# One of eight broadcast adds per pair of sequences on POOL instead of VectorE, with a copy of the keys in SBUF

## The reference, cut to what matters

```python
q = x @ Wq + bq
k = x @ Wk + bk
v = x @ Wv + bv
scores = einsum('d,bijd->bij', attn_scale, tanh(q[:, :, None, :] + k[:, None, :, :]))
weights = softmax(scores, axis=-1)
attn = einsum('bij,bjd->bid', weights, v)
attn = attn @ Wo + bo
x = layer_norm(x + attn, g1, beta1)
h = relu(x @ W1 + bf1)
x = layer_norm(x + h @ W2 + bf2, g2, beta2)
```

## Time and profile before

| | |
|---|---|
| median of three timed runs | 1179.35 us (1177.79 to 1180.16) |
| the profiled execution | 1169.94 us, its span 1168.1 us |
| pair stages (additive attention to routing) | from 0 to about 740 us |
| experts | about 760 to 1064 us |
| last stage | about 1064 to 1168 us |
| one turn in the loop, from one qT (406.54) to the next (447.44) | 40.90 us: DVE busy 35.59, PE 34.23, ACT 31.63, POOL 10.76 us |
| TensorE clock granted in that turn | 0.96 of full speed, mean of the span 0.909 |

### The profile page before, as it was taken

The page is one execution under the profiler, slowest core; times in us unless marked ns, Lnnn a source line. Parts: engine busy times, 40 slices in busy tenths (PEclk is TensorE's granted clock), DMA queues, the critical chain, the costliest instruction groups (busy, mean ns, idle before and its releaser), DMA issues.

```text
span 1168.1 us, 24664 instructions
## 1 busy us (share of the span) xinstructions
PE 872.7 (75%) x7427; PEld 665.8 (57%) x7427; DVE 708.7 (61%) x2209; ACT 667.8 (57%) x1643; POOL 392.2 (34%) x458
## 2 busy tenths in 40 slices
PE   3457889789778978987898887167766666665887
PEld 1235566556555655655665565166656656665787
DVE  4398878988898898889889643311211112123776
ACT  3266878777777877777787554033433434342343
POOL 7500111322331232233123333365655555551111
PEclk9978899999999999999998888578998998897999
DMA  8200000000000000000000000447766675665000
GB/s 196 29 1 1 1 8 2 8 8 0 7 7 7 0 7 7 0 7 7 7 0 8 8 8 8 90 131 212 210 183 193 182 196 169 179 185 112 14 17 21
DMA packets 53976, 71.08 MB, mean 61 GB/s; under 512 B 10818, under 2 KB 40624, under 8 KB 53936
## 3 DMA queue, kind: packets, MB, share of 16 engines
q1 hardware_dynamic: 45456, 62.56, 19.7%
q0 software_dynamic: 8480, 8.01, 3.0%
HBM read 64.17 MB, written 11.03 MB: 64 GB/s over the span
## 4 chain that ended last, share of the span: by engine, by line
PE 36%; issue 25%; DVE 19%; DMA 8%; another core or an unknown queue 5%; POOL 3%; SPq 2%; ACT 1%; DVEq 0%; POOLq 0%
PE b_s L1207 6%; DMA b2buf<-in_L_ffn_b 5%; PE big L1334 5%; PE b_o L1374 5%; DVE tbuf L794 5%; PE big L1486 4%; PE big L1324 4%; DVE spread L794 4%; POOL pr L424 2%; DVE pr L921 2%; PE b_qk L1501 2%; PE b_s L1501 2%; PE big L1361 1%; SPq L343 1%
## 5 line engine op out<-in xcount | busy, mean ns | idle before, releaser
L1486 PE MATMUL big<-hbT,wbuf 128*128 128x128 f32 x672 | 108.5, 312 | 91.7 <-DMA b2buf<-in_L_ffn_b 47.4
L794 DVE TENSOR_TENSOR tbuf<-qT,b_qk 128x2304 f32<-128x2304 f32 x64 | 162.7, 2547 | 19.6 <-remote 10.7
L657 ACT ACTIVATE act_h<-big,wbuf 128x128 f32<-128x128 f32 x336 | 95.7, 368 | 122.5 <-PE big L1486 75.7
L541 ACT ACTIVATE tbuf<-tbuf 128x2304 f32<-128x2304 f32 x64 | 135.6, 2119 | 46.6 <-DVE tbuf L794 38.4
L1486 PEld LDWEIGHTS big<-hbT,wbuf 128*128 128x128 f32 x672 | 94.0, 216 | 103.8 <-issue 50.7
L1207 PE MATMUL b_s<-tbuf,apad 128*32 128x192 f32 x1536 | 97.5, 393 | 59.4 <-ACT p L550 51.8
L1092 DVE TENSOR_SCALAR hbT<-b_t,cols 128x128 f32<-128x128 f32 x84 | 34.3, 409 | 147.8 <-PE b_t L1479 85.1
L482 POOL DMA_INDIRECT hrow<-tok_dram,igather x84 | 85.5, 1018 | 80.9 <-PE b_t L1479 37.4
L491 POOL DMA_INDIRECT eo_dram<-eo,iscatter x84 | 85.9, 1023 | 56.7 <-issue 32.7
L424 POOL TENSOR_TENSOR pr<-pr,rs 96x384 f32<-96x384 f32 x64 | 52.7, 824 | 149.5 <-DVE rs L928 149.5
L1207 PEld LDWEIGHTS b_s<-tbuf,apad 128*32 128x32 f32 x1536 | 51.0, 126 | 90.4 <-issue 48.8
(11 more groups left out here) (209 smaller groups left out, 1916.0 us busy)
## 6 DMA issues: line engine op xcount, KB each, us to landing
wbuf<-in_wpack SPq DMA_DIRECT2D x84, 514.0 KB
b2buf<-in_L_ffn_b SPq DMA_DIRECT2D x84, 64.0 KB
tok_dram<-tn SPq DMA_DIRECT2D x32, 96.0 KB
spread<-eo_dram SPq DMA_DIRECT2D x1, 2688.0 KB, 16.0
out<-of SPq DMA_DIRECT2D x16, 96.0 KB, 1.7
hrow<-tok_dram,igather POOLq DMA_INDIRECT x84
eo_dram<-eo,iscatter POOLq DMA_INDIRECT x84
tab_dram<-tid_now,slot_now POOLq DMA_INDIRECT x64
```

What stands on the lines that cost most here:

```text
L541: act.activation(v, v, ACT.Tanh).then_inc(s["tanh"], 1)
L657: last = act.activation(act_h[:, r % 2, c * TILE:(c + 1) * TILE], big[r % 2][:, c * TILE:(c + 1) * TILE], ACT.Silu, bias=wbuf[:, r, 2 * DF ...
L794: dve.tensor_tensor(ring[c % TRING].rearrange("p (x m n) -> p x m n", m=CQ, n=N), qv.unsqueeze(3).to_broadcast([D, SPLIT * QG, CQ, N]), kv ...
L1486: last = pe.matmul(big[r % 2][:, c * TILE:(c + 1) * TILE], wbuf[:, r, c * D:(c + 1) * D], hbT[:, r % 2, :], start=True, stop=True)
```

## The change

A new helper `add_chunk` writes the add for any engine and any copy of the keys. The last chunk of a pair, number 7 (LENT), goes to POOL. POOL can't read PSUM, so `qk_evac` first copies the keys to SBUF (`kT`). POOL's add stands right after `keep_x` in its body; it waits for the queries of its pair and for score 3, which frees its buffer. It counts on a semaphore of its own, `add_p`. The tanh of chunk 7 waits for that one, the other tanh for the DVE's count of seven a pair, and PE's `qk` and DVE's `qk_evac` wait for both.

```diff
--- before.py
+++ after.py
@@ -33,6 +33,7 @@
 CH = G * CPB
 CW = SPLIT * QG * CQ * N
 TRING = 4
+LENT = CH - 1
 DEPTH = 5
 VC = D + 2
 EPS_TOK, EPS = 1e-6, 1e-5
@@ -155,6 +156,7 @@
         xs = sb("xs", [N, G, D])
         xT = sb("xT", [D, TN])
         qT = sb("qT", [D, TN])
+        kT = sb("kT", [D, TN])
         bqk = sb("bqk", [D, 1])
         vrow = sb("vrow", [N, G, VC])
         nmax = sb("nmax", [128, SPLIT])
@@ -251,7 +253,7 @@
 
         s = {n: ctx.enter_context(nc.semaphore("s_" + n)) for n in [
             "ids", "ld_a", "ld_b", "late", "consts", "gate", "pool_c", "tab_init", "setup_mm", "setup",
-            "raw_mm", "raw_ev", "emb0", "emb1", "emb2", "xs", "kept", "xs_t", "xT", "qk", "qk_ev", "add", "tanh", "score",
+            "raw_mm", "raw_ev", "emb0", "emb1", "emb2", "xs", "kept", "xs_t", "xT", "qk", "qk_ev", "add", "add_p", "tanh", "score",
             "nmax", "exp1", "p1t", "p1T", "vp", "vp_ev", "att", "x1", "x1h", "x1_t", "x1T", "x1bT", "f", "f_ev", "y2",
             "x2", "h0_rows", "xa", "xa_t", "xaT", "hg", "hg_ev", "hv", "hv_ev", "s2", "s2_ev", "exp2", "rs2", "pn",
             "t2", "t2_ev", "o_init", "o", "h1n", "res", "tn", "tn_t", "hT", "r", "rT", "lg", "routed", "gap",
@@ -285,6 +287,17 @@
             return t[:, bass.ds(p, 1), :, :].rearrange("p a g d -> p (a g) d")
 
 
+        def add_chunk(eng, c, keys):
+
+            g, cc = c // CPB, c % CPB
+            qv = qT[:, g * N:(g + 1) * N].rearrange("p (x m) -> p x m", m=QM)[:, :, CQ * cc:CQ * cc + CQ]
+            kv = keys[:, g * N:(g + 1) * N]
+            return eng.tensor_tensor(
+                ring[c % TRING].rearrange("p (x m n) -> p x m n", m=CQ, n=N),
+                qv.unsqueeze(3).to_broadcast([D, SPLIT * QG, CQ, N]),
+                kv.unsqueeze(1).unsqueeze(1).to_broadcast([D, SPLIT * QG, CQ, N]), ALU.add)
+
+
         @block.sync
         def _(sp):
             def load(dst, src, sem):
@@ -409,6 +422,11 @@
                 pool.wait_ge(s["xs"], p + 1)
                 pool.tensor_copy(pair_of(res, p), xs[:, :, :]).then_inc(s["kept"], 1)
 
+            def add(p):
+                pool.wait_ge(s["qk_ev"], p + 1)
+                pool.wait_ge(s["score"], p * CH + LENT - TRING + 1)
+                add_chunk(pool, LENT, kT).then_inc(s["add_p"], 1)
+
             def root(p, n):
                 pool.wait_ge(s["var_" + n], p + 1)
                 pool.tensor_tensor(rstd[n][:, :], ve[n][:, :], neghalf[:, 0:G], ALU.pow)\
@@ -453,6 +471,7 @@
 
                 at(n, 1, root, "x1")
                 at(n, -1, keep_x)
+                at(n, 0, add)
 
                 at(n, 3, roots_h1)
                 at(n, 2, normalise, 0)
@@ -536,7 +555,10 @@
             act.preload_act_table(ACT.Exp)
 
             def tanh(p, c):
-                act.wait_ge(s["add"], p * CH + c + 1)
+                if c == LENT:
+                    act.wait_ge(s["add_p"], p + 1)
+                else:
+                    act.wait_ge(s["add"], p * (CH - 1) + c + 1)
                 v = ring[c % TRING]
                 act.activation(v, v, ACT.Tanh).then_inc(s["tanh"], 1)
 
@@ -782,20 +804,15 @@
 
             def qk_evac(p):
                 dve.wait_ge(s["qk"], p + 1)
-                wait(dve, s["add"], p * CH)
+                wait(dve, s["add"], p * (CH - 1))
+                wait(dve, s["add_p"], p)
+                dve.tensor_copy(kT[:, :], p_k)
                 dve.tensor_scalar(qT[:, :], b_qk[:, 0:TN], bqk[:, :], None, ALU.add).then_inc(s["qk_ev"], 1)
                 dve.wait_ge(s["qk_ev"], p + 1)
 
             def add(p, c):
                 wait(dve, s["score"], p * CH + c - TRING + 1)
-                g, cc = c // CPB, c % CPB
-                qv = qT[:, g * N:(g + 1) * N].rearrange("p (x m) -> p x m", m=QM)[:, :, CQ * cc:CQ * cc + CQ]
-                kv = p_k[:, g * N:(g + 1) * N]
-                dve.tensor_tensor(
-                    ring[c % TRING].rearrange("p (x m n) -> p x m n", m=CQ, n=N),
-                    qv.unsqueeze(3).to_broadcast([D, SPLIT * QG, CQ, N]),
-                    kv.unsqueeze(1).unsqueeze(1).to_broadcast([D, SPLIT * QG, CQ, N]), ALU.add)\
-                    .then_inc(s["add"], 1)
+                add_chunk(dve, c, p_k).then_inc(s["add"], 1)
 
             def x_rows(p):
                 if known(p) and p == 0:
@@ -1012,7 +1029,6 @@
                 at(n, 1, x1_norm)
                 at(n, 0, v_rows)
 
-                at(n, 0, add, 7)
                 at(n, 2, mask_max, 0)
 
                 at(n, 0, products)
@@ -1216,7 +1232,8 @@
 
             def qk(p):
                 pe.wait_ge(s["xT"], p + 1)
-                wait(pe, s["add"], p * CH)
+                wait(pe, s["add"], p * (CH - 1))
+                wait(pe, s["add_p"], p)
                 for i in range(2):
                     last = pe.matmul(b_qk[:, i * TN:(i + 1) * TN], wqk[:, i, :], xT[:, :], start=True, stop=True)
                 last.then_inc(s["qk"], 1)
```

## The result

| | before | changed kernel |
|---|---|---|
| median of four timed runs | 1179.76 us (1177.79 to 1182.27) | 1199.8 us (1194.96 to 1204.2) |
| the profiled execution | 1169.94 us | 1194.96 us |
| its span | 1168.1 us | 1193.1 us |
| mean granted TensorE clock | 0.909 | 0.887 |
| one turn in the loop, qT to qT | 40.90 us | 42.19 us |

The ratio is 1.0175, with a 95% interval of 1.0141 to 1.021: the change makes the kernel slower by about 20 us. The forecast was 1213.8 us, with a range of 1192 to 1238. Profile against profile the difference is 25.0 us, where the prediction summed 34.4.

What follows compares the result with a forecast made beforehand. The turn's path was taken to lie on PE up to `qk`, then on DVE. Stalls of `x1_norm` and `cums` of 30.35 us plus copies made 34.4 us, added to the 1179.35 us median: 1213.8 us, range 1192 to 1238.

Steps and rivals of the forecast that it cites:

- Add 7 is worth nothing: On PE's half of the turn: removing DVE's 2.54 us add only lengthens its 1.95 us wait to about 4.5 us.
- the adds are the bound after all: Rival, chance 0.04: DVE's add of chunk 7 would be on the path, its removal saving 2.27 us a turn, total 1145.
- the reading of the two halves of the turn: The turn's path lies on PE from the transposes behind `xa` to `qk`, then on DVE from the queries through adds 0 to 2.
- The copy, 15 x 0.27 = 4.05 us: On DVE between `qk` and the queries: copying the keys is all on the path, 0.27 us for each of pairs 1 to 15.
- POOL's add, 4.94 us: On POOL behind `keep_x`: the chunk's add sized as six times a 0.823 us operation of 384 values, hidden as work.
- the two bounds of 3.5 and 4.94: Length of POOL's add: 3.5 us from nine one-input copies of 0.39 us, 4.94 from six two-input operations of 0.823 us.
- x1_norm stands still until POOL is through: On DVE beside POOL's add: `x1_norm` takes some 3 us instead of 0.59, ending 0.34 us after the add.
- The term of 1.8 us a turn: PE starts `x1_turn` at 400.28 instead of 398.51 because `x1_norm` waits; turns 4, 6 to 14 and 15 give 19.8 us.
- Turn 5: POOL's add should start before the late `cums`, so `cums`, add 6 and `x1_norm` stand behind it: 4.4 us.
- POOL before `cums` in every turn: Rival, chance 0.11: POOL's add goes ahead of `cums` in turns 6 to 14 too, 23 us more, 1237.
- No stall: Rival, chance 0.12: `x1_norm` isn't held by POOL's add, so only the copies count: 1183.4 us.
- The clock falls in the new gap: Rival, chance 0.10: PE's clock falls after standing still 1.8 us before `x1_turn`, 2 us a turn, 22 more, 1236.

Runs made afterwards that it cites:

- POOL's add behind `x1_norm`: The changed kernel, with POOL's add also waiting until `x1_norm` of the turn is done: 1117.11 us, ratio 1.0014 to the kernel before.
- the same with the copy late: The changed kernel, with POOL's add waiting for `x1_norm` and for the keys' copy, which moves to where add 7 stood: 1112.69 us, ratio 0.9968 to the kernel before.
- Chunk 2's place: Against the kernel before, POOL adds chunk 2 instead of chunk 7, behind `roots_h1` and `slot_now`; DVE keeps chunk 7 and pair 0's chunk 2: 1157.51 us, ratio 0.9821.
- copy-only kernel: The kernel before plus the copy of the keys ahead of the queries, read by nobody; all eight adds stay on DVE: 1118.27 us against 1115.53, ratio 1.0036.
- the kernel with one input in PSUM: The changed kernel, with the roots copied to PSUM and `x1_norm` reading them there in another operation: 1182.59 us, ratio 1.0052 to the kernel before.
- the kernel that adds twice: The changed kernel, with POOL doing its add twice over the same buffer, writing the same values: 1212.55 us, ratio 1.0886 to the kernel before.

## Why the prediction came out right

- **Add 7 is worth nothing.** Right. The wait behind it grew from 1.95 to 3.95 us, and with the stall taken out (POOL's add behind `x1_norm`, and the same with the copy late) the turn is no shorter than before. The rival "the adds are the bound after all" fell for this place. Chunk 2's place showed the other half of it: there an add is worth 2.4 of its 2.54 us. This is what the reading of the two halves of the turn had said.
- **The copy, 15 x 0.27 = 4.05 us.** Right: 0.27 us a turn, and 2.7 us (medians) or 4.0 us (ratio) in the timed runs of the copy-only kernel.
- **POOL's add, 4.94 us.** The mis-sized term; it is 4.04 us. Six times the 0.823 us of the earlier trace rows is 4.94, and this counts their fixed part six times. A fixed part of 0.18 us and 1.68 ns a value would fit both 0.823 and 4.04, an estimate from two operations that differ in more than size. The add lies near the middle of the two bounds of 3.5 and 4.94. The rate of the Trainium skill's page (GPSIMD Engine Reference, "Elementwise — side-by-side cycle accounting") gave 5.06 us and is too high as well for this add: the trace has 1.76 ns a value, the page 2.20.
- **x1_norm stands still until POOL is through.** Right, in turns 1, 2, 4 and 6 to 15 and not in turn 3; in turn 5 `cums` and add 6 take its place. It ends 0.33 us behind POOL's add; 0.34 was said. With the form changed the stall is gone. The rule of the Trainium skill (SBUF — State Buffer, "Who interferes with whom") holds here for both kinds: add 6, with one input in PSUM, runs at 2.54 us beside POOL, and `x1_norm` waits.
- **Turn by turn.** The term of 1.8 us a turn inherits the 0.90 of POOL's add: 0.9 was due, and 1.02 was measured beside the copy (turns 6 to 14: 1.29 - 0.27). Turn 1 grew 2.98 beside the copy, against 3.55 forecast and 2.65 due; turn 2 grew 1.51 against 2.6 and 1.7. With the add at 4.04 the whole sum is 34.4 - 14 x 0.90 = 21.8 us. The measured 25.0 is 3.2 above: 2.0 in turn 5, mostly the clock; about 0.12 in each of the nine turns of 42.19 us, for the weight load of the transposes that no longer runs ahead; 0.4 in turn 12; and the others take some 0.3 back, among them turn 15, whose stall would be 0.9 with the shorter add, while all that comes behind pair 15's qT grew by 0.4.
- **Turn 5.** The order, POOL before `cums`, was forecast, and the kernel that makes POOL wait for `cums` showed it right. It hung on little, and the reason given for it, a `cums` that starts when the copy is over, isn't what the trace has: `cums` starts 0.12 us after the copy starts, in turn 5 as in the loop turn shown, and runs beside it in both. The price is 5.5 us beside the copy against 4.4 forecast and 3.5 due, because the clock fell behind 3.56 us of idle. The prediction had priced a fall of the clock only for the short gap of the other turns, where 0.71 us of idle brought none.
- **The rivals.** "POOL before `cums` in every turn" didn't occur: only turn 5 has it. "No stall" is refuted by the traces and by the kernel with one input in PSUM. "The clock falls in the new gap" came only in turn 5 (in turn 1 the transposes were slow before as well) and, with the gap made 4.58 us, in the kernel that adds twice.
- **The base.** The profiled execution of the changed kernel is its fastest timed run, 4.8 us below its median; that of the kernel before lay 9.8 below. So the medians are only 20.0 us apart and the profiles 25.0. The forecast is 14.0 us above the measured median: 12.6 is the length of POOL's add, 5.0 this difference, and the 3.2 us that the sum lacked, with 0.4 by which the median before moved, offset part of it. That the miss isn't larger is in this part luck. The 1193.6 that the prediction gave for an add of 3.5 us bounds it from below.

## What to carry to other kernels

Before an operation is moved to POOL, list the DVE instructions that read all their inputs from SBUF in the time that it will run. Here `x1_norm` and `cums` were held until POOL's add was through, while those with an input in PSUM passed. Not every POOL operation holds them so long: `oh`, with both inputs in SBUF, took 0.45 us beside a root of 0.72 us on POOL, and 0.42 with POOL idle. Whether the freed DVE time is worth anything depends on which engine owns the path at that place of the turn, not on which is busiest: of two equal adds one was worth nothing and the other 2.4 of 2.54 us. Price a long instruction between the rate of a short one and that of the cheapest kind, not at the sum of short ones.

## What was unexpected of the hardware

- Whether a waiting DVE instruction gets in between two POOL instructions goes with a gap of hundredths. In the kernel that adds twice, the adds last 4.04 us each of 8.17, so some 0.08 lie between them: the first half of `x1_norm` ended there, and the second half was held by the second add. In the loop turn shown above, too, 0.06 us lie between copy (to 411.38) and add (from 411.44), and `cums` ended at 411.46. In turn 5 the add's row starts at 238.29, before the copy's ends at 238.32, and `cums` was held by the add as well. What goes with the gap is score 3 (the rows of `b_s<-wbuf` above), for which the add waits: it ends at 411.32 (410.14 + 1.18) in the loop turn, just before the copy does, and at 238.04 (236.86 + 1.18) in turn 5, well before. Three places in agreement don't show the mechanism.
- POOL's two-input add of 2304 values with both inputs broadcast takes 1.76 ns a value; the scaling of 384 values 2.14 ns, both with their fixed part.
- A stall of DVE can reach PE's clock. PE kept it through 0.71 us of idle, and in the kernel before through 2.09, and had it at half for some 3.4 us behind 3.56 and behind 4.58 us, which cost 1.7 us each time.
